# Two-layer attention, gate, scan and FFN kernel on one core: the first batch's score tiles 4 to 7 taken from fetched bf16 parts instead of fp32 keys, and two FFN waits of layer 2 stated more narrowly

## What is computed

```python
xn = layernorm(x)                        # x: 8 batches x 256 tokens x 128
x = x + attention(xn) + gated_relu_ffn(xn)          # layer 0
xn = layernorm(x)
x = x + scan_block(xn) + ternary_ffn(xn)            # layer 1 of the reference
# attention: 16 heads of size 8, 4 key heads; softmax(q k / sqrt(8)) v, then @ Wo
# ternary_ffn: silu(x w1) * (x w2) -> gelu(. h1) -> gelu(. h2) -> . w3, hidden width 512
```

## Time and profile before

| | us |
|---|---|
| median of 3 runs (lowest to highest) | 357.62 (357.30 to 357.71) |
| the profiled execution, whole | 357.89 |
| its span, first to last instruction | 356.10 |
| TensorE (PE) busy | 348.4 |
| VectorE (DVE) busy | 307.3 |
| ScalarE (ACT) busy | 291.1 |
| GpSimd (POOL) busy | 232.6 |

### The profile page before, as it was taken

One profiled execution on the slowest core, in us unless ns is written; L12 is line 12 of the kernel. 1 busy time (PEld: TensorE's weight loads), 2 busy tenths in 40 slices (PEclk: granted clock), 3 DMA queues, 4 the chain that ended last, 5 costly groups with the idle time before them and its releaser, 6 DMA issues.

```text
span 356.1 us, 5750 instructions
## 1 busy us (share of the span) xinstructions
PE 348.4 (98%) x1754; PEld 181.6 (51%) x1754; DVE 307.3 (86%) x530; ACT 291.1 (82%) x508; POOL 232.6 (65%) x294
## 2 busy tenths in 40 slices
PE   7999999999999999999999999999999999999996
PEld 5556544747565523443444447444457444564446
DVE  5898889988899886499999999999999989799940
ACT  3875976877787885898899999999999999899620
POOL 0484457214420601344999989999898999999980
PEclk9999999999999999999999999999999999999999
DMA  4455776586724003000000000000000200000000
GB/s 167 130 146 119 146 204 143 81 131 196 197 78 74 6 0 123 22 1 2 0 0 23 3 0 24 15 0 1 1 2 0 67 0 1 2 0 1 31 0 29
DMA packets 28943, 19.26 MB, mean 54 GB/s; under 512 B 4241, under 2 KB 27889, under 8 KB 28657
## 3 DMA queue, kind: packets, MB, share of 16 engines
q1 hardware_dynamic: 28912, 18.90, 21.8%
HBM read 13.32 MB, written 5.37 MB: 53 GB/s over the span
## 4 chain that ended last, share of the span: by engine, by line
PE 87%; issue 5%; DVE 4%; POOL 2%; ACT 1%; POOLq 0%
PE bank L1028 15%; PE bank L1016 13%; PE bank L435 6%; PE bank L422 5%; PE bank L467 4%; PE bank L399 4%; PE bank L459 4%; PE bank L1005 4%; PE bank L1099 4%; PE bank L1006 4%; PE bank L989 4%; PE bank L1072 3%; PE bank L1052 3%; POOL acc L1368 2%; PE bank L388 2%
## 5 line engine op out<-in xcount | busy, mean ns | idle before, releaser
L1368 POOL TENSOR_TENSOR acc<-acc,hb 128x512 f32<-128x512 f32 x128 | 158.2, 1273 | 19.2 <-DVE hb L1312 18.9
L1312 DVE TENSOR_TENSOR_SCAN hb<-da,bank 128x512 f32<-128x512 f32 x128 | 146.0, 1200 | 9.2 <-PE bank L989 9.1
L680 DVE TENSOR_REDUCE mx<-bank 128x2 f32<-128x512 f32 x128 | 81.7, 682 | 7.2 <-PE bank L399 5.9
L1217 ACT ACTIVATE da<-dt,nega 128x510 f32<-128x510 f32 x128 | 81.4, 710 | 0.3 <-DVE da L1336 0.2
L1016 PE MATMUL bank<-sil,ld 128*128 128x512 f32 x128 | 59.5, 593 | 0.0
L1028 PE MATMUL bank<-gelu,ld 128*128 128x512 f32 x128 | 58.0, 592 | 0.0
L630 ACT ACTIVATE pt<-bank 128x512 f32<-128x512 f32 x72 | 39.6, 602 | 6.2 <-PE bank L422 4.5
L422 PE MATMUL bank<-q_st,k_st 51*128 51x512 bf16 (+1 forms) x128 | 39.8, 382 | 0.4
L1028 PEld LDWEIGHTS bank<-gelu,ld 128*128 128x128 f32 x128 | 24.3, 190 | 26.8 <-issue 25.4
L399 PE MATMUL bank<-k_st,q_st 48*128 48x256 bf16 x240 | 36.9, 272 | 0.0
L1016 PEld LDWEIGHTS bank<-sil,ld 128*128 128x128 f32 x128 | 24.0, 190 | 24.6 <-issue 22.9
(11 more groups left out here) (166 smaller groups left out, 527.3 us busy)
## 6 DMA issues: line engine op xcount, KB each, us to landing
q_st<-q_scr SPq DMA_DIRECT2D x15, 192.0 KB, 3.8
q_st<-q_scr SPq DMA_DIRECT2D x7, 384.0 KB, 5.3
ld<-in_pack SPq DMA_DIRECT2D x2, 1024.0 KB, 5.5
q_scr<-qk_parts SPq DMA_DIRECT2D x8, 192.0 KB, 2.5
k_st<-k_scr SPq DMA_DIRECT2D x14, 96.0 KB, 4.5
q_scr<-qk_parts SPq DMA_DIRECT2D x8, 128.0 KB, 2.7
out<-x SPq DMA_DIRECT2D x8, 128.0 KB, 2.0
ld<-in_pack SPq DMA_DIRECT2D x1, 968.0 KB, 7.6
```

The costliest lines, as they stand in the source:

```text
L680: eng.tensor_reduce(mx[:, 2 * pair:2 * pair + 2, q], score_bank(b, n)[:, :].rearrange("p (h k) -> p h k", h=2), AX.X, ALU.max).then_inc(mx ...
L1217: act(da(n)[:, :, 1:T], dt[:, g % 2, c, :].rearrange("p (b n) -> p b n", b=GB)[:, :, 1:T], ACT.Exp, scale=nega[:, c, s:s + 1]).then_inc(da ...
L1312: eng.tensor_tensor_scan(hb[:, s % NPAIR, c, :], da(n).rearrange("p b n -> p (b n)"), b_bank(g, s)[:, :], 0.0, ALU.mult, ALU.add).then_inc ...
L1368: TT(acc[:, g % 2, c, :], acc[:, g % 2, c, :], hb[:, s % NPAIR, c, :], ALU.add).then_inc(add_ok, 1)
```

## The change

Four things change.

- A constant NOWN = 4 takes the place of NH // 2 = 8: only the tiles n < 4 of batch 0 come from fp32 keys.
- The fetch of batch 0 brings key heads 1 to 3 (72 KB instead of 48 KB) and has one more DMA, query heads 4 to 7 (96 KB), ahead of the one with heads 8 to 15. Both count in sc0_ok, and tile n = 4 now waits for both (32), where tile n = 8 had waited for the keys (16).
- ScalarE's order loses two of its four own_keys. All other orders stay as they are.
- For g > 0, second's first halves for c = 0 and 1 wait for three hidden chunks instead of four, and third's first halves wait for max(2, c + 1) instead of four; the second halves, which waited for nothing, now wait for all four, for g = 0 too.

```diff
     scalar="""...
-        2*normalised 2*xn_out own_keys k_out own_keys q_out deviation0 relu gate_exp normalised xn_out normalised
+        2*normalised 2*xn_out k_out q_out deviation0 relu gate_exp normalised xn_out normalised
...
+NOWN = 4
...
             if b == 0:
-                k_rows(NKV // 2, NKV).then_inc(sc0_ok, 16)
+                k_rows(NOWN // G, NKV).then_inc(sc0_ok, 16)
             else:
...
             if b == 0:
                 reached(eng, scr_ok, b, 16 * NRUN, 16 * NRUN)
+                q_rows(NOWN, NH // 2).then_inc(sc0_ok, 16)
             q_rows(NH // 2, NH).then_inc(sc2_ok[b % 2], 16)
...
-            if b == 0 and n < NH // 2:
+            if b == 0 and n < NOWN:
...
-            if b == 0 and n == NH // 2:
-                eng.wait_ge(sc0_ok, 16)
+            if b == 0 and n == NOWN:
+                eng.wait_ge(sc0_ok, 32)
...
         def second(g, n):
             c, half = n // 2, n % 2
-            if half == 0:
-                reached(eng, h0_ok, g, KC, KC)
-                if g == 0:
-                    eng.wait_ge(done["ld"][2], 16)
-                    reached(eng, lift2_ok, g, 2, c - 1)
+            reached(eng, h0_ok, g, KC, KC - 1 if g > 0 and c < 2 and half == 0 else KC)
+            if half == 0 and g == 0:
+                eng.wait_ge(done["ld"][2], 16)
+                reached(eng, lift2_ok, g, 2, c - 1)
...
         def third(g, n):
             c, half = n // 2, n % 2
-            if half == 0:
-                reached(eng, g2_ok, g, KC, KC)
-                if g == 0:
-                    eng.wait_ge(done["ld"][3], 16)
-                    reached(eng, lift3_ok, g, 2, c - 1)
+            reached(eng, g2_ok, g, KC, max(2, c + 1) if g > 0 and half == 0 else KC)
+            if half == 0 and g == 0:
+                eng.wait_ge(done["ld"][3], 16)
+                reached(eng, lift3_ok, g, 2, c - 1)
```

More of the change, by code:

```diff
@@ L97 @@
     scalar="""roots deviation0 xn_out deviation0 wide_out q_out k_out own_keys normalised own_keys relu xn_out
-        2*normalised 2*xn_out own_keys k_out own_keys q_out deviation0 relu gate_exp normalised xn_out normalised
-        q_out relu xn_out normalised relu negated_maxima gate_exp normalised xn_out E xn_out 2*E k_out 2*E q_out 4*E
-        negated_maxima relu 2*E gate_exp relu 5*E q_out 6*E o_out E q_out 2*E negated_maxima 3*E gate_exp 4*E o_out
-        5*E relu 3*E relu negated_maxima 8*E gate_exp o_out 4*E q_out relu 2*E relu 2*E negated_maxima 3*E q_out relu
@@ L102 @@
[L102 to L106, removed]
@@ L107 @@
-        4*gelu 2*dt x_out 4*D taps 7*D taps 3*D 4*hid gate_x sil gate_z gate_x sil gate_z b_in 5*D 2*sil 16*D gelu D
-        3*gelu 2*dt 15*D 4*hid 2*sil 4*D 2*sil 7*D gelu 2*D 3*gelu 4*D 4*hid""",
+        2*normalised 2*xn_out k_out q_out deviation0 relu gate_exp normalised xn_out normalised q_out relu xn_out
+        normalised relu negated_maxima gate_exp normalised xn_out E xn_out 2*E k_out 2*E q_out 4*E negated_maxima relu
+        2*E gate_exp relu 5*E q_out 6*E o_out E q_out 2*E negated_maxima 3*E gate_exp 4*E o_out 5*E relu 3*E relu
@@ new lines @@
+        negated_maxima 8*E gate_exp o_out 4*E q_out relu 2*E relu 2*E negated_maxima 3*E q_out relu 2*E gate_exp relu
+        3*E decay_rates 2*E gate_exp 3*E o_out 2*E negated_maxima 3*E relu E relu 3*E deviation 4*E o_out 3*E gate_exp
+        relu 3*E negated_maxima 2*E relu 2*E x_out 3*E taps 8*E o_out 3*E gate_x E sil 4*E negated_maxima E sil taps
+        gate_z gate_x sil E b_in gate_z E o_out 2*dt 2*D x_out E sil D E taps D E 2*D taps D E 2*D E gate_x gate_z D
+        gate_x 2*E b_in gate_z D E D E 3*D E 2*D E 3*D 3*E 3*D o_out 2*D 4*gelu 2*dt 10*D deviation hid normalise hid
@@ L109 @@
+        x_out 2*hid 2*taps gate_x 2*sil gate_x 2*gate_z 2*D b_in 2*sil 16*D normalise 7*D 4*gelu 2*dt x_out 4*D taps
+        7*D taps 3*D 4*hid gate_x sil gate_z gate_x sil gate_z b_in 5*D 2*sil 16*D gelu D 3*gelu 2*dt 15*D 4*hid 2*sil
+        4*D 2*sil 7*D gelu 2*D 3*gelu 4*D 4*hid""",
     vector="""clear_values ones moments inverse moments wide_q inverse first_split v_out first_split 2*M
```

## The result

The changed kernel takes **362.31 us**, the median of 4 runs from 359.45 to 363.40, against 357.66 before (357.30 to 358.01, 4 runs). The ratio is 1.0116 with a 95% interval of 1.0095 to 1.0136: slower by 1.2%, clear of the noise. Forecast were 358.1 and a range up to 359.1. The profiled execution is one of 363.40 us, with a span of 361.6.

A forecast was written before the change was run, and what follows sets the result against it. DVE's row of maxima from 18.6 to 28.5 us was taken as the bound. Tile 4's maximum 0.6 us later, less 0.1 for slack, gave +0.5, all else 0: from 357.62 to 358.1 us, range 357.4 to 359.1.

The forecast's parts named there:

- What bounds this stretch: From 18.6 to 28.5 us DVE's row of maxima is tight; PE's 2.5 us less work gains nothing.
- The hold of tile 4: Tile 4 waits for fetched queries, landing 2.4 us after 16.30; its maximum starts at 19.21 instead of 18.60, 0.6 us later.
- rival 1: Queries land late, 3.0 us after issue: maximum of tile 4 at 19.81, +1.2 us, total 358.8; chance 0.37.
- Rival 3: TensorE's clock falls after PE's pause from 16.9 to 18.8 us: 5 us at half speed, +2.5, total 360.6; chance 0.03.
- Own_keys at nothing: Two ACT calls of 0.90 us removed, costed at nothing because DVE's layernorm aggregates hold what follows.
- the layer's waits at nothing: Narrowed and added waits in second and third, from 200 us on: 0; bounds a 1.3 us gain or no loss.
- Passing the loss on: Tile 4's 0.6 us moves through max_rows and the first A to the end nearly in full, less 0.1 for slack: +0.5.
- If warm matmuls behind the hole take 421 ns, it was the clock: Sign in the profile after: warming matmuls took 421 ns at 1.2 GHz and 273 ns at 2.4 GHz.

The follow-up runs named there:

- nine pieces: Changed kernel plus nine warming pieces (each two 128x256 bf16 matmuls, result unread) between query product and tile 4: 358.24 us against 357.68 for the kernel before.
- the old waits: Changed kernel with the second layer's waits as before, so the score tiles' change alone: 360.69 us against 357.68 for the kernel before.
- the filling behind: Changed kernel, pause left open, eight pairs of unread bf16 matmuls behind tiles 6, 7 and 8: 361.73 us against 357.70 for the kernel before.
- swapped reads: Changed kernel with query heads 4 to 7 of batch 0 read before the keys, no filling: 360.87 us against 357.70 for the kernel before.
- NOWN = 6: Changed kernel with tiles 4 and 5 again from fp32 keys, one own_keys back on ScalarE, no filling: 357.31 us against 357.65 for the kernel before.
- 15 pieces: Changed kernel, own read order, unread bf16 matmul pairs: nine in the pause, six behind tiles 6 to 8: 358.47 us against 357.65 for the kernel before.
- the swapped reads and six pieces: Changed kernel, query heads 4 to 7 read before the keys, six pairs of unread bf16 matmuls in the pause: 358.27 us against 357.70 before.

## Why the prediction was wrong

- **What bounds this stretch: right.** PE's 2.5 us less gave nothing, and the maximum of tile 4 set the row that follows. With nine pieces and the clock up, 0.56 us of idle time on DVE before it stand again at max_rows (+0.57).
- **The hold of tile 4: right in mechanism, and its size varies around the forecast.** 0.09 us from landing to the first matmul was 0.04, and 0.42 us from there to the maximum was 0.42. The landing, taken as 2.4 us, was 2.7 in the profiled run after and 2.2 to 2.4 in five others that fetch in this order. The read, taken to be issued at the same 16.30, went out at 16.65 in the profiled run. So there the maximum started at 19.81, which is the figure of rival 1; with the later layernorm taken off that is a loss of 1.1 us, not 0.6. In the six profiled executions with this order DVE is idle before the maximum for 0.29 to 0.99 us, and 0.56 in two of them. With the order of the reads swapped, the six executions at clock 1.000 take 357.2 us, against 357.7 before: no loss is left.
- **Rival 3, the clock: this is the step that failed.** It had a chance of 0.03, the sum put it at nothing, and it happened in every execution. I set it low "against it: the chain before the hole is full of matmuls". The runs say otherwise: with the hole open and short tiles behind it the clock fell in all sixteen executions (the changed kernel, with the old waits, with the filling behind, with swapped reads). And I looked only at the pause. But it is followed by six tiles of 0.21 us each, by what their matmuls take back to back. Four of them stand in place of fp32 matmuls of some 0.9 us, and the last three wait for maxima, which come one in 0.6 us. From 17.0 to 22.3 us PE issues only 1.3 us of matmuls, an estimate from these 0.21 us. I had written down both, that PE cannot use what it saves and that the tiles are paced by M, and did not put them together: saving time on PE where another engine sets the pace is what makes it idle.
- **Its price: mis-sized too.** I took 5 us at half speed and 2.5 us. It is 10 us at half speed in the profiled run, and 4.1 us of the median (362.31 - 358.24). The median execution too stands at 0.986. Ten microseconds at half speed could cost 5; I take it that DVE's row covers the rest, which no run separates. It is large because ffn_out (2.05 to 3.78 us) and the projections lie on the chain behind the thin tiles.
- **The page TensorE: Matmul & The Clock Gate** of the Trainium skill (section on the clock gate) says that the clock halves after the array has been idle. The traces agree with the fall to 0.50. They show that it needs no unbroken pause: it also fell in six of twelve executions in which the pause was filled and only the thin tiles were left.
- **Own_keys at nothing, the layer's waits at nothing: right.** The second by a run of its own, the first only in that nothing of ACT's 0.9 us shows.
- **Passing the loss on: right for the large loss, open for the small one.** In the changed kernel it is +5.3 at max_rows, +4.8 at the first A, +5.5 at the end. With nine pieces it is +0.57 at max_rows and about half of that at A. The DMA queue has a part in it. Before, one write of SyncE between the rows of maxima took 1.70 us in the queue, the last row was issued behind it, and A started 0.5 us behind the score tile ahead of it (33.46 and 33.96). After, the write took 0.58 us, the row had landed at 38.07, and A followed that tile at once (38.72 and 38.73):

```profile
30.33 1.70 SPq L295 DMA_DIRECT2D q_scr<-qk_parts  x1
...
35.65 0.58 SPq L296 DMA_DIRECT2D q_scr<-qk_parts  x1
```

  From max_rows to that tile it is 5.58 us in both, so this is the 0.5 us between max_rows and A. With NOWN = 6 the write took 0.58 us too, and A came 5.63 us behind max_rows instead of 6.08; that is likely where this kernel gains. Why the write is held up in the one and not in the other was not tested.
- **"If warm matmuls behind the hole take 421 ns, it was the clock"** was the right thing to look for, and the profile's clock row answers it at once.

Open: what exactly decides between 1.000, 0.995, 0.990 and 0.986, and how pause and thin stretch share in it. The pause with three short tiles behind it was enough in two traces, the thin tiles with the pause filled in one. Several of the kernels gave two or three of these values, and one execution of the kernel with 15 pieces took 360.72 at a clock of 1.000, which is not explained either.

## What to carry to other kernels

Before taking work from TensorE, ask what it will do with the time: if another engine sets the pace there, the saving becomes idle time, and that can cost more than the work did, by the clock of all that follows. Add up what PE still issues over the whole thin stretch, pause and paced tiles together, and look at PEclk first when a kernel turns slower than its waits explain. Here two fp32 tiles left on PE did best (357.3 us), since they also gave DVE its first maxima on time; matmuls that compute nothing came next (358.2), and the open pause last (362.3).

## What the runs showed of the hardware that I had not expected

- The clock's fall differs from execution to execution of one and the same kernel: with the swapped reads and six pieces, twelve executions gave 1.000 six times, 0.995 four times and 0.986 twice, and 357.2, 359.2 and 362.5 us. A median of few runs can land on any of them.
- What comes behind a pause counts as well as its length: 2.1 us with four fp32 tiles behind it left the clock at 0.995 or more in all four executions; 1.5 us with the thin tiles behind it brought it to 0.986 to 0.990 in all four. Warming pieces behind the pause did not save it: 0.986 to 0.995.
- A write of 64 KB to DRAM at 21.5 us landed in 1.5 us before, 3.8 us after and 3.5 us with nine pieces, and in 1.7 us with 15 pieces. I don't know why. In the profile after, the queries of batch 1 were fetched at 25.41 instead of 23.01, behind a wait of 2.3 us for this write.
